# One adaLN transformer layer in split fp32r products: the second copy of k's high parts by DMA, and pair 0 of the heads split too

## The chip, the cores and the metric

The kernel runs on one core of a Trainium2 chip. The metric is the device time of one execution in microseconds; smaller is better. The core has TensorE (PE, with its weight loads shown apart as PEld), VectorE (DVE), ScalarE (ACT), GpSimd (POOL) and SyncE (SP, which here only issues DMAs). Every engine works through its own list of instructions in order and waits on semaphores.

## The reference, cut to what matters

There are 16 batches of 256 tokens with 128 features, 16 query heads of 64, and 4 key and value heads (4 query heads share one).

```
h = layernorm(x) * (1 + ca) + sa
q, k, v = h @ Wq, h @ Wkv;  q, k = rotary(q), rotary(k)
attn = softmax(q @ k.T / 8)               # per head, 256 x 256
x = x + ga * ((attn @ v) @ Wo + bo)
h = layernorm(x) * (1 + cb) + sb
x = x + gb * (gelu(h @ bin(w1).T + b1) @ bin(w2).T + b2)
```

`bin(w)` is the sign of w times the mean of its absolute values by row; `ga` and `gb` are made from a small conditioning matrix.

## The kernel before, in words

All work is float32 or float32r (a reduced float32 that TensorE multiplies faster). Where plain precision is wanted of float32r, an operand is cut into a **high** part (its value rounded to float32r) and a **low** part (the rest), and the product is made of high times high, high times low and low times high.

**Steps.** `attention_steps` (L155 to L166) runs one step for each batch, with the projections of the next batch (`prep`) and the output projection of the batch before (`out`) in the same step. There are 16 steps with attention, one ahead of them that only prepares, and a tail. The feed-forward part follows (`mlp_step`), partly beside the tail. All engines run the same step bodies.

**Slots.** A step has eight slots, and `SLOTS` (L60 to L69) is an order of work written by hand: slot 0 is

```
"S0 s4 s5 m s6 m s7 xT0 xT0 m m S1 m qt4 qt4 m mT1 qt4 qt4",
"S0 m s8 S1 m qkv02 qt5 qt5 qt5 qt5 qkv12 m m m m",
```

with slot 1 under it. PE goes through the words in order. ACT, DVE and POOL go through the same words and do what follows from each on their engine; of a unit that has several parts they act at its last word. A word is one of these:

- `S0`, `S1`: the transposed scores of one pair of heads (pair = slot number), one half of the keys each (`scores`, L962 to L976): two fp32r products, L972 and L974, into one of two banks `score_ps`. ACT then takes the exponential into `probs` (L648), and for a pair in `SPLIT_PAIRS` (L131) once more into `probs_hi` (L651); POOL makes `probs_lo` by subtraction (L515).
- `m`: one part of the product of the pair *of the slot before* with v (`product_with_v`, L978 to L1002), six words a pair. A plain pair uses the first and the fourth word only, with one plain fp32 product each (L989). A split pair uses all six with one fp32r product each (L999), two of `probs_hi` with `v_hi`, two with `v_lo`, two of `probs_lo` with `v_hi`; the last two wait for POOL. `SPLIT_PAIRS` is (1, 3, 4, 5, 7), so pairs 0, 2 and 6 are plain.
- `kt0`, `kt1`, `qt0` to `qt7`: PE turns k and q by identity products (L926). ACT copies q into `q_hilo` (L582), and k's high part **twice**, into the lower and the upper 64 partitions of `k_hi2` (the loop over `half` at L576 and L577), and its low part into `k_lo1` (L579). The upper copy is there because q's high and low parts lie on 128 partitions and both meet k's high part.
- `s0` to `s15`: one head's scores (L937), of which DVE takes the row maxima (L758); `s8` is the first to use `qt4` and waits for it (L933); `s0` and `s8` also wait for `k_hi2` (L934, L935). `mT0` to `mT3`: the maxima of four heads are turned (L941), and ACT copies them (L589).
- `qkv..`: projections (L911 to L913), then rotary terms on DVE (L748, L750), POOL (L501, L505) and ACT (L600). `xT0`: the normalised tokens turned (L903), then ACT (L564, L567) and DVE (L734).
- `bc..`, `yT..`, `zT0`: the reciprocals of the softmax sums spread by a product (L947) and applied on DVE (L763), the output projection (L953), and its turning back. `recip0` and `recip1` are DVE's reciprocals (L776 to L781).

A slot begins on ACT with the copy `o_un` of a finished pair (L657). Units use four banks `unit_ps` in turn; a unit waits for the reader of the one four before (`wait_for_reader`, L869).

**SP's list** in a step (L442 to L460) is: `maxima` of quarter 1, `gather_sums` 1, `high_parts` 2, `spread_reciprocals` 1, `maxima` 2, `high_parts` 3, `maxima` 3, `gather_sums` 0, `spread_reciprocals` 0, then for the next batch `high_parts` 0, `maxima` 0, `high_parts` 1. `high_parts` copies q's high parts of four heads into `q_him` (L419, 256 KB), `maxima` puts the turned maxima beside them (L425), `gather_sums` and `spread_reciprocals` lay the softmax sums and their reciprocals out over partitions (L432, L439). Each waits for what it copies and holds up what stands behind it.

Of the kernel before, what the change touches and what calls it, by code (L numbers as in the profile page):

```python
# [29 lines left out]
F32 = mybir.dt.float32  # L30
# [5 lines left out]
P = 128  # L36
# [91 lines left out]

SIGNS_AT = 4

SPLIT_PAIRS = (1, 3, 4, 5, 7)  # L131


class Step:
# [128 lines left out]
def adaln_layer(nc, x, wq, wkv, wo, bo, w1, b1, w2, b2, c, wmod, cos, sin, out):  # L263
    ctx = ExitStack()
    with ctx:
# [109 lines left out]
            sem("v_hi_ready"), sem("rot_parts"), sem("rot_summed"), sem("rot_high"), sem("rot_ready"))  # L375
        k_hi_ready, k_lo_ready, q_ready = sem("k_hi_ready"), sem("k_lo_ready"), sem("q_ready")
        q_him_in = [sem(f"q_him_in{i}") for i in range(4)]
        ident_r_ready, select_ready = sem("ident_r_ready"), sem("select_ready")
        neg_max_zero, max_ready, max_t_ready = sem("neg_max_zero"), sem("max_ready"), sem("max_t_ready")
        scores_full, probs_ready, pv_done = sem("scores_full"), sem("probs_ready"), sem("pv_done")  # L380
# [15 lines left out]
        @block.sync  # L396
        def _(sp):
            sp.dma_start(c_sb[:, :], c).then_inc(c_in, 16)
            sp.dma_start(xa[:, 0, :, :], x[0].rearrange("(c p) d -> p c d", p=P)).then_inc(x0_in, 16)
            sp.dma_start(wmod_sb, wmod).then_inc(wmod_in, 16)  # L400
            sp.dma_start(w_all[:, 0:INNER], wq).then_inc(wq_in, 16)
            sp.dma_start(w_all[:, INNER:WIDE], wkv).then_inc(wq_in, 16)
            sp.dma_start(cos_sb[:, :, :], cos.rearrange("(c p) d -> p c d", p=P)).then_inc(rope_in, 16)
            sp.dma_start(sin_sb[:, :, :], sin.rearrange("(c p) d -> p c d", p=P)).then_inc(rope_in, 16)
            sp.dma_start(bo_sb[:, :], bo.rearrange("(p o) -> p o", o=1)).then_inc(bias_in, 16)
            sp.dma_start(b2_sb[:, :], b2.rearrange("(p o) -> p o", o=1)).then_inc(bias_in, 16)
            for k in range(KF):
                sp.dma_start(b1_sb[:, k:k + 1], b1[k * P:(k + 1) * P].rearrange("(p o) -> p o", o=1)).then_inc(bias_in, 16)
            sp.dma_start(w1_sb[:, :, :], w1.rearrange("(k p) d -> p k d", p=P)).then_inc(ffw_in, 16)
            sp.dma_start(w2_sb[:, :], w2).then_inc(ffw_in, 16)  # L410
            for b in range(1, B, 5):
                sp.dma_start(xa[:, b:b + 5, :, :], x[b:b + 5].rearrange("b (c p) d -> p b c d", p=P)).then_inc(x_in, 16)
            sp.dma_start(wo_sb[:, :, :], wo.rearrange("(s p) n -> p s n", p=P)).then_inc(wo_in, 16)

            def high_parts(st, quarter, batch):


                sp.wait_ge(q_ready, st.count(8, 2 * quarter + 2, batch))
                sp.dma_start(q_him[quarter % 2][0:DH, :, :].bitcast(F32),  # L419
                             q_hilo[st.par(batch)][0:DH, 4 * quarter:4 * quarter + 4, :].bitcast(F32)).then_inc(q_him_in[quarter], 16)  # L420

            def maxima(st, quarter, batch):

                sp.wait_ge(max_t_ready, st.count(4, quarter + 1, batch))
                sp.dma_start(q_him[quarter % 2][DH:DH + 1, :, :].bitcast(F32).rearrange("o h (c i) -> o (h c) i", c=C),  # L425
                             neg_max_t[quarter % 2][:, :].bitcast(F32)).then_inc(q_him_in[quarter], 16)

            def gather_sums(st, half, batch):


                sp.wait_ge(o_un_ready, st.count(8, 4 * half + 4, batch))
                sp.dma_start(sums[:, :], o_un[DH:DH + 1, 4 * half:4 * half + 4, :, :]  # L432
                             .rearrange("o s h (b t) -> o (s h b) t", t=16)).then_inc(sums_in[half], 16)

            def spread_reciprocals(st, half, batch):

                sp.wait_ge(recip_lo_ready, st.count(2, half + 1, batch))
                for first, part in ((0, recip_hi), (32, recip_lo)):
                    sp.dma_start(recip_parts[half][first:first + PAIRS, :].bitcast(F32).rearrange("h (b t) -> h b t", t=16),  # L439
                                 part[:, :].bitcast(F32)).then_inc(recip_in[half], 16)  # L440

            def step(st):  # L442
                if st.attn:
                    maxima(st, 1, 0)
                if st.out:
                    gather_sums(st, 1, -1)
                if st.attn:
                    high_parts(st, 2, 0)
                if st.out:
                    spread_reciprocals(st, 1, -1)  # L450
                if st.attn:
                    maxima(st, 2, 0)
                    high_parts(st, 3, 0)
                    maxima(st, 3, 0)
                    gather_sums(st, 0, 0)
                    spread_reciprocals(st, 0, 0)
                if st.prep:
                    high_parts(st, 0, 1)
                    maxima(st, 0, 1)
                    high_parts(st, 1, 1)  # L460

            attention_steps(sp, step)

            with sp.Fori(0, B // 2) as t:
                for odd in range(2):
                    sp.wait_ge(y_ready, t * 2 + (odd + 1))
                    sp.dma_start(out[bass.ds(t * 2 + odd, 1)].rearrange("b (c p) d -> p (b c) d", p=P),
                                 y_sb[odd][:, :, :]).then_inc(y_out[odd], 16)
            for odd in range(2):
                sp.wait_ge(y_out[odd], 16 * (B // 2))  # L470
# [72 lines left out]
        def _(act):  # L543
# [12 lines left out]
            def unit(st, place, u):  # L556
                kind, ps, par = u[0], (tail_ps if st.tail else unit_ps)[bank(st, place)], st.par(ahead(u))
                if kind in ("s", "zT", "bc") or (kind == "qkv" and u[2] != 2) or u == ("yT", 0):
                    return
                act.wait_ge(unit_full, nth_unit(st, place))  # L560
                if kind == "xT":

                    b = st.batch(1)
                    act.activation(h_t[:, :], ps[:, 0:N], ACT.Identity, scale=mod[:, 1, bass.ds(b, 1)],  # L564
                                   bias=mod[:, 0, bass.ds(b, 1)]).then_inc(h_ready, 1)
                    act.wait_ge(h_ready, st.count(1, 1, 1))
                    act.activation(h_hi[0][:, :], h_t[:, :], ACT.Copy).then_inc(h_hi_ready, 1)  # L567
                if kind == "qkv":
                    act.activation(v_whole[par][:, u[1], :, 0:DH],
                                   ps[:, 256:512].rearrange("p (g d) -> p g d", g=KV), ACT.Copy)  # L570
                    act.activation(v_hi[par][:, u[1], :, 0:DH],
                                   ps[:, 256:512].rearrange("p (g d) -> p g d", g=KV), ACT.Copy).then_inc(v_hi_ready, 1)
                if kind == "kt":

                    high = ps[0:DH, :].rearrange("p (g i) -> p g i", g=2)
                    for half in range(2):  # L576
                        act.activation(k_hi2[par][half * DH:half * DH + DH, 2 * u[1]:2 * u[1] + 2, :], high,  # L577
                                       ACT.Copy).then_inc(k_hi_ready, 1)
                    act.activation(k_lo1[par][0:DH, 2 * u[1]:2 * u[1] + 2, :],  # L579
                                   ps[DH:P, :].rearrange("p (g i) -> p g i", g=2), ACT.Copy).then_inc(k_lo_ready, 1)  # L580
                if kind == "qt":
                    act.activation(q_hilo[par][:, 2 * u[1]:2 * u[1] + 2, :],  # L582
                                   ps[:, :].rearrange("p (h i) -> p h i", h=2), ACT.Copy).then_inc(q_ready, 1)
                if kind == "mT":
                    quarter = u[1]
                    if st.number != (-1, 0, None, None)[quarter]:

                        act.wait_ge(q_him_in[(quarter - 2) % 4], st.count(32, -32 if quarter < 2 else 0, ahead(u) + 1))
                    act.activation(neg_max_t[quarter % 2][:, :], ps[0:4 * C, 0:P], ACT.Copy).then_inc(max_t_ready, 1)  # L589
                if kind == "yT":  # L590

                    b = st.batch(-1)
                    act.activation(z_sb[:, :], ps[:, 0:N], ACT.Identity, scale=mod[:, 2, bass.ds(b, 1)],
                                   bias=ga_bo[:, bass.ds(b, 1)]).then_inc(z_ready, 1)
# [263 lines left out]
        def _(pe):  # L858
# [32 lines left out]
            def unit(st, place, u, part, last):  # L891
# [37 lines left out]
                if kind == "s":  # L929
# [2 lines left out]
                    if h % 2 == 0:  # L932
                        pe.wait_ge(q_ready, st.count(8, h // 2 + 1, ahead(u)))  # L933
                    if h % 8 == 0:  # L934
                        pe.wait_ge(k_hi_ready, st.count(4, h // 4 + 2, ahead(u)))  # L935
                    for ch in range(C):
                        ins = pe.matmul(ps[:, ch * N:(ch + 1) * N], q_hilo[par][:, h, ch * P:(ch + 1) * P],  # L937
                                        k_hi2[par][:, g, :], start=True, stop=True)
# [167 lines left out]
```

## Time and profile before

| what | value |
|---|---|
| median of 3 runs (711.74 to 713.76) | 713.3 us |
| the profiled execution, its own time | 712.71 us |
| its span in the profile | 710.9 us |
| PE busy | 672.1 us, 95% of the span |
| ACT busy | 551.4 us, 78% |
| DVE busy | 515.1 us, 72% |
| POOL busy | 430.6 us, 61% |
| mean granted TensorE clock | 0.978 |

The span is what the trace shows; 1.8 us of the execution's own time lie around it. A matmul's row starts when it enters the array's pipeline and ends when its last result is out, so neighbouring rows overlap, and the distance between two starts is what a matmul costs. A plain fp32 matmul stands as two rows.

### The profile page before, as it was taken

Reading aid. Unit: us, or ns where it says so; the run is one execution under the profiler, and the core shown is the slowest. Engines: PE = TensorE matmul, PEld = TensorE weight load, DVE = VectorE, ACT = ScalarE, POOL = GpSimd, SP = SyncE. Lnnn points to the kernel's source line nnn. Section 1 sums busy time; section 2 is a strip of 40 time slices with the busy share of each in tenths; the row PEclk is TensorE's granted clock in tenths of the full one; section 3 lists DMA queues with packets and bytes.
Section 4 is the critical chain, followed back from the end, with each engine's and each line's share of the span. In section 5 each row is a group of like instructions: output and inputs, shape, how many; then the busy total and the mean of one; then the engine's idle time right before and its main releaser. Section 6 shows DMA issues by size and latency. Waiting matters only on the chain.

```text
span 710.9 us, 13528 instructions
## 1 busy us (share of the span) xinstructions
PE 672.1 (95%) x3733; PEld 523.1 (74%) x3733; DVE 515.1 (72%) x1195; ACT 551.4 (78%) x1148; POOL 430.6 (61%) x397
## 2 busy tenths in 40 slices
PE   3488999999999999999999999999999999997897
PEld 3366777777878787878777777778777878666786
DVE  5556787887777777777787878777777777657673
ACT  3558887878788788878788878787887878766586
POOL 0447675867767676858576758577676768452110
PEclk9679999999999999999999999999999999998999
DMA  8011111111111111110201111111101111100111
GB/s 239 13 31 31 33 33 32 32 34 31 28 30 22 31 31 32 29 33 16 46 17 31 31 32 31 31 31 31 30 18 32 31 34 32 33 17 9 31 38 45
DMA packets 31580, 24.75 MB, mean 35 GB/s; under 512 B 16688, under 2 KB 26944, under 8 KB 31552
## 3 DMA queue, kind: packets, MB, share of 16 engines
q1 hardware_dynamic: 31552, 24.40, 16.3%
q8 instruction: 14, 0.23, 0.1%
q14 instruction: 14, 0.11, 0.1%
HBM read 4.47 MB, written 2.10 MB: 9 GB/s over the span
## 4 chain that ended last, share of the span: by engine, by line
PE 89%; DVE 3%; ACT 2%; issue 1%; POOL 1%; DMA 1%; SPq 0%; DVEq 0%; POOLq 0%
PE o_ps L999 15%; PE o_ps L989 11%; PE unit_ps L937 9%; PE score_ps L972 8%; PE score_ps L974 8%; PE unit_ps L926 8%; PE unit_ps L953 8%; PE o_ps L1054 4%; PE unit_ps L911 3%; PE unit_ps L912 3%; PE unit_ps L913 3%; PE unit_ps L947 2%; PE unit_ps L941 2%; DVE o_t L763 1%; PE unit_ps L1032 1%
## 5 line engine op out<-in xcount | busy, mean ns | idle before, releaser
L515 POOL TENSOR_TENSOR probs_lo<-probs,probs_hi 128x512 fp32r<-128x512 f32 x160 | 202.4, 1284 | 72.5 <-ACT probs_hi L651 72.5
L758 DVE TENSOR_REDUCE w_all<-unit_ps 128x2 f32<-128x512 f32 x256 | 166.0, 685 | 51.9 <-PE unit_ps L937 50.4
L501 POOL TENSOR_TENSOR rot_sum<-rot_a,rot_b 128x512 f32<-128x512 f32 (+1 forms) x96 | 104.8, 1098 | 106.7 <-DVE rot_b L750 106.5
L648 ACT ACTIVATE probs<-score_ps 128x512 f32<-128x512 f32 x256 | 150.5, 588 | 20.6 <-PE score_ps L974 18.0
L505 POOL TENSOR_TENSOR qk_rot<-rot_sum,qk_rot 128x512 fp32r<-128x512 f32 (+1 forms) x96 | 105.1, 1102 | 36.0 <-ACT qk_rot L600 36.0
L937 PEld LDWEIGHTS unit_ps<-k_hi,q_hilo 128*128 128x128 f32 x512 | 89.1, 192 | 42.8 <-issue 18.5
L937 PE MATMUL unit_ps<-k_hi,q_hilo 128*128 128x256 f32 x512 | 118.3, 319 | 2.1 <-ACT q_hilo L582 1.6
L972 PE MATMUL score_ps<-q_hilo,k_hi 128*128 128x512 f32 x256 | 113.4, 443 | 1.6 <-DMA q_him<-neg_max_t 1.6
L926 PEld LDWEIGHTS unit_ps<-ident_r,qk_rot 128*128 128x128 f32 x640 | 102.0, 194 | 16.9 <-issue 4.6
L926 PE MATMUL unit_ps<-ident_r,qk_rot 128*128 128x128 f32 x640 | 109.7, 263 | 4.5 <-POOL qk_rot L505 4.2
L763 DVE TENSOR_TENSOR o_t<-o_un,unit_ps 64x256 f32<-64x256 f32 x248 | 103.5, 417 | 5.7 <-PE unit_ps L947 1.3
L974 PE MATMUL score_ps<-q_him,k_lo 65*128 65x512 f32 x256 | 102.0, 398 | 0.0
L989 PE MATMUL o_ps<-probs,v_whole 128*65 128x512 f32 x192 | 98.1, 592 | 0.0
L651 ACT ACTIVATE probs_hi<-score_ps 128x512 fp32r<-128x512 f32 x160 | 94.1, 588 | 0.0
L582 ACT ACTIVATE q_hilo<-unit_ps 128x512 fp32r<-128x512 f32 x128 | 76.2, 596 | 8.5 <-PE unit_ps L926 8.3
L657 ACT ACTIVATE o_un<-o_ps 65x512 f32<-65x512 f32 x128 | 74.3, 581 | 1.9 <-PE o_ps L999 1.0
L748 DVE TENSOR_TENSOR rot_a<-unit_ps,cos_sb 128x512 f32<-128x512 f32 (+1 forms) x96 | 57.2, 596 | 24.0 <-PE unit_ps L941 16.8
L972 PEld LDWEIGHTS score_ps<-q_hilo,k_hi 128*128 128x128 f32 x256 | 48.8, 191 | 16.9 <-issue 9.3
L999 PE MATMUL o_ps<-probs_hi,v_hi 128*65 128x512 f32 x160 | 60.3, 395 | 0.0
L999 PE MATMUL o_ps<-probs_hi,v_lo 128*65 128x512 f32 x160 | 59.8, 411 | 0.0
L953 PE MATMUL unit_ps<-o_t,wo_sb 128*128 128x128 f32 x480 | 59.4, 277 | 0.0
L600 ACT ACTIVATE qk_rot<-rot_sum 128x512 fp32r<-128x512 f32 (+1 forms) x96 | 52.3, 561 | 8.5 <-POOL rot_sum L501 8.5
(119 smaller groups left out, 1128.7 us busy)
## 6 DMA issues: line engine op xcount, KB each, us to landing
q_him<-q_hilo SPq DMA_DIRECT2D x64, 256.0 KB
out_x<-w_all SPq DMA_DIRECT2D x16, 128.0 KB, 1.8
xa<-in_L_attn_x SPq DMA_DIRECT2D x3, 640.0 KB, 7.6
q_him<-neg_max_t SPq DMA_DIRECT2D x64, 4.0 KB
w_all<-in_L_attn_Wq SPq DMA_DIRECT2D x1, 512.0 KB, 4.4
w_sb<-in_L_ffn_w SPq DMA_DIRECT2D x2, 256.0 KB, 2.9
wo_sb<-in_L_attn_Wo SPq DMA_DIRECT2D x1, 512.0 KB, 7.8
sums<-o_un SPq DMA_DIRECT2D x32, 8.0 KB, 2.1
```

Source lines behind the costliest of these rows:

```text
L505: pool.tensor_tensor(low, total, high.bitcast(F32), ALU.subtract).then_inc(rot_ready, 1)
L515: pool.tensor_tensor(probs_lo[s % 2][:, jc, :, :], probs[s % 2][:, jc, :, :], probs_hi[s % 2][:, jc, :, :].bitcast(F32), ALU.subtract).the ...
L648: ins = act.activation(probs[s % 2][:, jc, :, :].rearrange("p h i -> p (h i)"), score_ps[jc][:, :], ACT.Exp, scale=SCALE)
L758: dve.tensor_reduce(neg_max[u[1] // 4][:, first:first + C], ps[:, :].rearrange("p (c j) -> p c j", c=C), AX.X, ALU.max, negate=True).then_ ...
L763: ins = dve.tensor_tensor(o_t[h * DH:h * DH + DH, u[1], :], o_un[0:DH, u[1], h, :], ps[h * DH:h * DH + DH, 0:N], ALU.mult)
L926: ins = pe.matmul(ps[:, part * P:(part + 1) * P], qk_rot[:, ch, first + h, :, :].rearrange("p t d -> p (t d)"), ident_r[:, :], start=True, ...
L937: ins = pe.matmul(ps[:, ch * N:(ch + 1) * N], q_hilo[par][:, h, ch * P:(ch + 1) * P], k_hi2[par][:, g, :], start=True, stop=True)
L953: ins = pe.matmul(ps[:, own], wo_sb[:, s, :], o_t[:, s, own], start=s == 0, stop=s == PAIRS - 1)
L972: pe.matmul(ps[:, :], k_hi2[par][:, g, js], q_hilo[par][:, hs, :].rearrange("p h i -> p (h i)"), start=True, stop=False)
L974: pe.matmul(ps[:, :], k_lo1[par][:, g, js], q_him[s // 2 % 2][:, s % 2 * 2:s % 2 * 2 + 2, :].rearrange("p h i -> p (h i)"), start=False, s ...
L989: ins = pe.matmul(o_ps[i][0:DH + 1, :], v_whole[par][:, jc, g, :], probs[i][:, jc, :, :].rearrange("p h i -> p (h i)"), start=jc == 0, sto ...
L999: ins = pe.matmul(o_ps[i][0:DH + 1, :], v[par][:, jc, g, :], p[i][:, jc, :, :].rearrange("p h i -> p (h i)"), start=part == 0, stop=part == 5)
```

## The change

`SPLIT_PAIRS` gets pair 0. ACT writes k's high part once, to the lower 64 partitions, and SP copies it to the upper 64 by one DMA for each of kt0 and kt1, with semaphores of their own. On SP's list the two DMAs stand behind `maxima` 3 and ahead of `gather_sums` 0. `s0` and `s8` wait for them instead of ACT's copies. A split pair's waits on POOL count 12 for a step in place of 10.

```
-SPLIT_PAIRS = (1, 3, 4, 5, 7)
+SPLIT_PAIRS = (0, 1, 3, 4, 5, 7)
...
+        k_twice_in = [sem(f"k_twice_in{i}") for i in range(2)]
...
+            def double_high_k(st, half, batch):
+
+                sp.wait_ge(k_hi_ready, st.count(2, half + 1, batch))
+                sp.dma_start(k_hi2[st.par(batch)][DH:P, 2 * half:2 * half + 2, :].bitcast(F32),
+                             k_hi2[st.par(batch)][0:DH, 2 * half:2 * half + 2, :].bitcast(F32)).then_inc(k_twice_in[half], 16)
...
                     maxima(st, 2, 0)
                     high_parts(st, 3, 0)
                     maxima(st, 3, 0)
+                if st.prep:
+                    double_high_k(st, 0, 1)
+                    double_high_k(st, 1, 1)
+                if st.attn:
                     gather_sums(st, 0, 0)
                     spread_reciprocals(st, 0, 0)
...
-                    for half in range(2):
-                        act.activation(k_hi2[par][half * DH:half * DH + DH, 2 * u[1]:2 * u[1] + 2, :], high,
-                                       ACT.Copy).then_inc(k_hi_ready, 1)
+                    act.activation(k_hi2[par][0:DH, 2 * u[1]:2 * u[1] + 2, :], high, ACT.Copy).then_inc(k_hi_ready, 1)
...
-                        pe.wait_ge(k_hi_ready, st.count(4, h // 4 + 2, ahead(u)))
+                        pe.wait_ge(k_twice_in[h // 8], st.count(16, 16, ahead(u)))
```

## Rows read from the trace of the kernel before

**Rows 1.** The page: busy times, and the chain that ended last by engine

```profile
PE 672.1 (95%) x3733; PEld 523.1 (74%) x3733; DVE 515.1 (72%) x1195; ACT 551.4 (78%) x1148; POOL 430.6 (61%) x397
...
PE 89%; DVE 3%; ACT 2%; issue 1%; POOL 1%; DMA 1%; SPq 0%; DVEq 0%; POOLq 0%
```

**Rows 2.** The chain in order of time, slots 1 and 2: start, length, what

```profile
311.14 0.86 PE o_ps L989 x2
312.00 0.24 PE unit_ps L937 x2
...
316.11 0.23 PE o_ps L999
```

**Rows 3.** Timeline, ACT in slot 0 and into slot 1: start, length

```profile
309.02 0.56 ACT L564 ACTIVATE h_t<-unit_ps,mod 128x256 f32<-128x256 f32 x1 [1.48 <-PE unit_ps L903]
...
309.94 0.58 ACT L648 ACTIVATE probs<-score_ps 128x512 f32<-128x512 f32 x1
...
310.56 0.27 ACT L589 ACTIVATE neg_max_t<-unit_ps 8x128 fp32r<-8x128 f32 x1
...
310.74 0.57 ACT L582 ACTIVATE q_hilo<-unit_ps 128x512 fp32r<-128x512 f32 x1
...
311.69 0.57 ACT L648 ACTIVATE probs<-score_ps 128x512 f32<-128x512 f32 x1
...
312.17 0.57 ACT L651 ACTIVATE probs_hi<-score_ps 128x512 fp32r<-128x512 f32 x1
```

**Rows 4.** Timeline: PE waits for q in slot 0; its products in slot 1

```profile
306.00 0.58 ACT L582 ACTIVATE q_hilo<-unit_ps 128x512 fp32r<-128x512 f32 x1
...
306.72 0.53 PEld L937 LDWEIGHTS unit_ps<-k_hi,q_hilo 128*128 128x128 f32 x4 [0.41 <-ACT q_hilo L582]
...
307.30 0.40 PE L999 MATMUL o_ps<-probs_hi,v_hi 128*65 128x512 f32 x1
...
310.98 1.02 PE L989 MATMUL o_ps<-probs,v_whole 128*65 128x512 f32 x2
...
312.07 0.40 PE L972 MATMUL score_ps<-q_hilo,k_hi 128*128 128x512 f32 x1
```

**Rows 5.** Timeline of the step after: the same exponential, q copy and L972

```profile
347.62 0.58 ACT L648 ACTIVATE probs<-score_ps 128x512 f32<-128x512 f32 x1
...
348.40 0.60 ACT L582 ACTIVATE q_hilo<-unit_ps 128x512 fp32r<-128x512 f32 x1
...
349.84 0.39 PE L972 MATMUL score_ps<-q_hilo,k_hi 128*128 128x512 f32 x1
```

**Rows 6.** Timeline, POOL from slot 0 to slot 1

```profile
307.88 1.29 POOL L505 TENSOR_TENSOR qk_rot<-rot_sum,qk_rot 128x512 fp32r<-128x512 f32 x1
312.82 2.54 POOL L515 TENSOR_TENSOR probs_lo<-probs,probs_hi 128x512 fp32r<-128x512 f32 x2 [3.66 <-ACT probs_hi L651]
```

**Rows 7.** Timeline, slots 4 to 6: ACT's k copies, SP's issues, DVE's reciprocals

```profile
327.26 1.22 ACT L577 ACTIVATE k_hi<-unit_ps 64x512 fp32r<-64x512 f32 x2
...
331.26 0.68 SPq L425 DMA_DIRECT2D q_him<-neg_max_t  x1
...
332.06 0.55 SPq L432 DMA_DIRECT2D sums<-o_un  x1
...
334.13 0.26 DVE L776 RECIPROCAL recip<-sums 128x16 f32<-128x16 f32 x1 [0.62 <-DMA sums<-o_un]
...
334.82 2.54 POOL L515 TENSOR_TENSOR probs_lo<-probs,probs_hi 128x512 fp32r<-128x512 f32 x2
...
334.92 1.22 DVE L780 TENSOR_TENSOR recip_lo<-recip,recip_hi 128x16 fp32r<-128x16 f32 x1
...
336.55 0.69 DVE L758 TENSOR_REDUCE w_all<-unit_ps 128x2 f32<-128x512 f32 x1 [0.41 <-PE unit_ps L937]
...
337.61 0.53 SPq L419 DMA_DIRECT2D q_him<-q_hilo  x1
```

**Rows 8.** By windows: busy PE, PEld, DVE, ACT, POOL; clock; DMA share, GB/s

```profile
339.00:339.50 0.50, 0.50 (x3) 0.32 (x2) 0.50 (x2) 0.00 (x0) 0.50 (x1) 1.00 1.09 213
```

## The prediction, made before the change was run

> **What bounds the kernel now.** I read the page first: PE is busy 95% of the span and makes 89% of the chain that ended last [rows 1], so only what changes PE's order of work in time counts. The same eight slots come back in each of 16 steps, so I then read one step: the chain in order of time [rows 2], and beside it the timelines of ACT, PE and POOL around slots 0 and 1, where the changed products stand [rows 3, 4, 6], the same place one step later [rows 5], and slots 4 to 6, where the copies of k stand [rows 7, 8]. The reader is to see two things. In slots 0 and 1 PE is never idle in the chain. But the work that PE waits for there comes only just in time: the q copy that s8 needs ends on ACT at 311.31 (310.74 + 0.57) [rows 3], while PE is still in pair 0's plain product, which began at 310.98 and holds it until s8 starts, 0.24 ahead of the L972 at 312.07 [rows 2, 4]. The slow product hides ACT.
>
> All sums below are made against the profiled execution, 712.71 us, of which 710.9 are its span. It stands 0.6 under the median of the runs, 713.3, and inside their spread.
>
> **PE's work.** Removed in a step: two plain products of pair 0, at 0.86 each in the chain, 1.72. Added: six fp32r products at 0.23, 1.38 [rows 2]. PE has 0.34 less to do, 5.4 in 16 steps. By the Trainium skill, FP8 and Floating Point Precision, section TensorE Precision Notes, true fp32 takes four passes of the array; two products would then be worth eight of the 0.23 passes, not 7.5 of them (1.72 / 0.23), and PE's relief would be 0.46 a step, 7.4 in all, by an estimate from that page. I keep the measured 0.86.
>
> **Where that work stands.** The first plain product stands ahead of s8, the second behind it. After the change one part stands ahead of s8 (0.23) and five behind it (5 x 0.23 = 1.15 in place of 0.86, so 0.29 more). So PE is 0.63 early at s8, and what counts is whether s8's operand is there.
>
> **ACT ahead of s8.** Pair 0 now needs a second exponential for each half of the keys. The first half's lies in the 1.48 that ACT idles ahead of h_t at 309.02 [rows 3]: nothing, and 0.48 if that idle time were gone. The second half's comes directly behind the exponential at 309.94, and ahead of the maxima's copy and the q copy that s8 waits for. Two exponentials follow each other at 0.48 (311.69 and 312.17). So: probs_hi at 310.42, the maxima's copy at 310.90, the q copy 0.18 behind it (310.56 to 310.74) at 311.08, done at 311.65 [rows 3].
>
> **From there to PE.** In slot 0 of the step PE does wait for a q copy, which gives the price: the copy ends at 306.58 and the load starts at 306.72, 0.14 later; four matmuls of L937 then take 0.58 until the next start at 307.30, the first load being bare, so two take 0.34 (0.58 less 0.24) [rows 2, 4]. So s8's load starts at 311.79 and the L972 behind it at 312.13, against 312.07 now: 0.06 late. In the step after, the exponential starts at 347.62, so the q copy at 348.76 (+0.48 + 0.48 + 0.18), ends at 349.36, and L972 starts at 349.84, just as now [rows 5]. Steps of these two kinds alternate; mean 0.03 late. The 0.63 that PE gained ahead of s8 is all waited away.
>
> **Behind s8.** The 0.29 more is then in the open, since nothing in the chain there but PE ends a wait. A step gets 0.03 + 0.29 = 0.32 longer; 16 steps give 5.1. Bounds: the link from q copy to L972 as measured, 0.48 in all, could be 0.1 shorter or longer in this place, 0.22 to 0.42 a step, so 3.5 to 6.7.
>
> **Part 0's own wait.** It now waits for the second probs_hi, which ends at 310.99 (310.42 + 0.57), so its load is at 311.13, against 310.98 for the product now [rows 3, 4]. It takes 0.23 and is done well ahead of s8's 311.79: nothing, and it would cost 0.15 if s8 did not wait longer.
>
> **ACT after s8.** ACT is 0.34 late (311.08 against 310.74), and its next work follows scores that PE makes 0.03 to 0.32 late itself; both move together, and I cost it at nothing. Behind it stand the o_un copy, slot 1's exponentials and SP's maxima of quarter 1; the latter are first used in slot 2, and I cost that at nothing too.
>
> **POOL.** Two more subtractions a step, 1.27 each (2.54 for two), 41 in 16 steps, on an engine that is busy 430.6 [rows 1, 6]. POOL is done with L505 at 309.17 and idles until 312.82. The first subtraction runs from 309.17 to 310.44, the second from about 311.1, when its probs_hi is there, to 312.4; the products that use them stand last in slot 1, nine fp32r products of 512 columns behind the L972 at 312.13 (part 1, six of the projections, parts 2 and 3), so not ahead of 314.2. Nothing on the path; up to 1.27 if POOL were not idle there. DVE's h_lo comes to lie beside the first subtraction and may be held up by it, up to 1.27, as recip_lo is in [rows 7]; it is not used before slot 1's first projection, so nothing.
>
> **The k copies.** ACT loses two copies of 0.61 a step (1.22 for two) [rows 7]. ACT's row count so stays as it was: two exponentials come for two copies, in other slots. ACT is 2% of the chain [rows 1], and in slots 4 and 5 of the steps I read PE follows PE, so this relief is worth nothing on PE; a gain is not excluded, and I bound it by that 2%, 14 us, of which I take nothing because none of it lies in these slots. SP gets two issues between the maxima of quarter 3 (331.26) and the sums (332.06). The nearest row is the copy of q's high parts, 256 KB in one issue of 0.53 [rows 7], moved at 213 GB/s [rows 8], so 1.2; the two k copies together carry as many bytes. Two issues put the sums back by 1.06; but the maxima's copy and o_un on ACT, which SP waits for, come 1.22 earlier. So the maxima are issued at 330.04, the k copies from 330.72, the sums at 331.8, 0.3 ahead of now, and they may queue behind the 1.2 of the k copies: they land between 333.9 and 334.5, where DVE now has them at 334.13 (332.06 + 2.07). DVE has 0.41 idle behind its reciprocals [rows 7], so nothing. The k copies themselves are issued by 331.8 and, at the sums' 2.07 and their own 1.2, land by 335.1 at the latest; s0's maxima start at 336.55, and s8 is in the next step: nothing. Without ACT's 1.22 the sums would be 1.06 late or more, which is the last rival.
>
> **Sum.** 712.7 + 5.1 = 717.8: slower, by 0.7%. Own range 715.5 to 720.
>
> **Rivals.** *Faster:* s8 finds its q copy ready, and PE keeps its 0.34 a step: 712.7 - 5.4 = 707.3. It decides at the q copy's end: to keep all, that must come by 310.7 or so (311.31 less 0.63). For it speaks that PE is 89% of the chain and has less to do. Against it, even today's 311.31 is too late. The Trainium skill's four passes would make this rival 705.3, by an estimate from the same page; the trace's 0.86 speaks against it.
>
> *No change:* ACT's extra exponential is hidden and q ends at 311.31 as now. Then the load is at 311.45 and L972 at 311.79, 0.28 early; with the 0.29 behind it the step is as long as before: 712.9. The timeline speaks against it [rows 3], since only 0.04 lies between the exponential's end (310.52) and the next start. What ACT is relieved of in slots 4 and 5 could give it no more here, since it idles 1.48 in between.
>
> *Slower still:* the sums are late after all, by the 1.06 of two issues or more. DVE's recip_lo takes 1.22 at 334.92 and ends with POOL's first subtraction (334.82 + 1.27 = 336.09); starting over 1.06 later, it would meet the second and end at 337.36, and the maxima that start at 336.55 would be 0.8 late [rows 7]. The Trainium skill, SBUF — State Buffer, section Summary: rules for kernel authors, says that of a DVE operation with two SBUF inputs and a GpSimd one the later blocks until the other is finished; the row agrees. Between 0 and 0.8 a step of it reaches PE; with 0.4 and 16 steps, 717.8 + 6.4 = 724.2. That the two DMAs don't do what ACT's copies did is no separate case: if they come late, s0 waits, and this rival prices it.
>
> **Chances.** Forecast 0.68; no change 0.14; faster 0.11; slower still 0.07. A measurement of this kernel tells 0.3%, 2.1 us, from no change. Some of the forecast's low end and all of the no-change case fall within it. So faster 0.11, same 0.16, slower 0.73. The range leaves out the faster rival and the slowest case, and takes in no change: 711.5 to 722.
>
> **What would show it.** Right: L989 loses a third of its rows, L999 and POOL's L515 gain a fifth; in slot 1 PE's load of L937 waits for ACT's L582, 16 times and some 0.5 each; a step takes 38.0 in place of 37.68 (309.94 to 347.62) [rows 3, 5]; the sums land as before. Wrong: no wait on L582 at s8 and a shorter step (the faster rival); a wait for DVE's L758 or for sums in slots 5 and 6 (slower still); a wait for POOL's L515 or for the k copy, which I cost at nothing.

## The result, and the profile after

| kernel | median | ratio to the kernel before | 95% interval |
|---|---|---|---|
| before | 712.83 us | | |
| after | 717.09 us | 1.0064 | 1.0048 to 1.0079 |

The change made the kernel slower by 0.6%, some 4.3 us by the medians. The profiled execution after took 716.65 us with a span of 714.9, which is 3.9 and 4.0 more than before; the granted clock was 0.978 in both.

The page of the kernel after: busy times, the chain by engine, three groups of instructions (busy, mean ns, idle before) and one DMA issue.

```profile
PE 672.7 (94%) x3765; PEld 526.9 (74%) x3765; DVE 516.4 (72%) x1195; ACT 546.1 (76%) x1148; POOL 470.6 (66%) x429
...
PE 84%; ACT 6%; DVE 3%; issue 3%; POOL 1%; DMA 1%; SPq 0%; ACTq 0%; DVEq 0%; POOLq 0%
...
L526 POOL TENSOR_TENSOR probs_lo<-probs,probs_hi 128x512 fp32r<-128x512 f32 x192 | 243.5, 1284 | 35.8 <-ACT probs_hi L660 35.8
...
L1008 PE MATMUL o_ps<-probs_hi,v_hi 128*65 128x512 f32 x192 | 73.5, 398 | 0.1
...
L998 PE MATMUL o_ps<-probs,v_whole 128*65 128x512 f32 x128 | 65.4, 592 | 0.0
...
k_hi<-k_hi SPq DMA_DIRECT2D x32, 128.0 KB, 2.2
```

Against [rows 1], ACT has 5 us less to do, but went from 2% of the chain to 6%, and "issue" from 1% to 3%: the span holds waits that it did not hold before. POOL has 40 us more.

Timeline of the kernel after, slots 0 and 1 of the step that [rows 3, 4] show of before (all lines stand 9 higher: L981 is the L972 of before, L946 the L937, L1008 the L999).

```profile
311.52 0.39 PE L981 MATMUL score_ps<-q_hilo,k_hi 128*128 128x512 f32 x1
...
311.58 1.28 POOL L526 TENSOR_TENSOR probs_lo<-probs,probs_hi 128x512 fp32r<-128x512 f32 x1
...
312.40 0.58 ACT L657 ACTIVATE probs<-score_ps 128x512 f32<-128x512 f32 x1
...
312.53 0.61 DVE L743 TENSOR_TENSOR h_lo<-h_t,h_hi 128x256 fp32r<-128x256 f32 x1
...
312.88 0.59 ACT L660 ACTIVATE probs_hi<-score_ps 128x512 fp32r<-128x512 f32 x1
...
313.36 0.25 ACT L598 ACTIVATE neg_max_t<-unit_ps 8x128 fp32r<-8x128 f32 x1
...
313.51 0.57 ACT L591 ACTIVATE q_hilo<-unit_ps 128x512 fp32r<-128x512 f32 x1
...
313.59 0.13 PEld L1008 LDWEIGHTS o_ps<-probs_hi,v_hi 128*65 128x65 f32 x1 [0.44 <-issue]
...
314.21 0.30 PEld L946 LDWEIGHTS unit_ps<-k_hi,q_hilo 128*128 128x128 f32 x2 [0.48 <-issue]
314.21 0.49 PE L946 MATMUL unit_ps<-k_hi,q_hilo 128*128 128x256 f32 x2 [0.17 <-ACT q_hilo L591]
...
314.54 0.40 PE L981 MATMUL score_ps<-q_hilo,k_hi 128*128 128x512 f32 x1
...
315.01 0.40 PE L1008 MATMUL o_ps<-probs_hi,v_hi 128*65 128x512 f32 x1
```

The new exponential stands at 312.88 between the old one and the maxima's copy. The q copy follows at 313.51 and ends at 314.08, and s8's load starts at 314.21: PE waited, both for part 0's operand (313.59) and for s8's (314.21). The view puts these waits of the loads down to "issue", because here an instruction of PE's sequencer ahead of the load carries the wait: the one with the wait for q starts at 314.121, 0.04 behind the copy's end. The same stretch before:

```profile
309.06 0.39 PE L972 MATMUL score_ps<-q_hilo,k_hi 128*128 128x512 f32 x1
```

From this product of slot 0 to slot 1's own (312.07 in [rows 4]) PE took 3.01; after it takes 314.54 - 311.52 = 3.02, with 0.63 less work in it. In the steps between it takes 3.02 before and 2.87 after.

To compare kernels I take the length of a step: the distance between the starts of xT0's second product in the fourth and in the fourteenth step that has one, over ten. The ten steps hold both kinds in equal number. Each ratio stands against runs of the kernel before on the same chip: 712.83 us for after, 713.28 for e1, e2, e3 and e5, 712.26 for e4, e6, e7 and e8, 712.72 for e9 and e8b.

| kernel | starts, us | step, us | median, us | ratio (95%) |
|---|---|---|---|---|
| before | 119.76, 497.17 | 37.74 | | |
| after | 120.73, 501.35 | 38.06 | 717.09 | 1.0064 (1.0048 to 1.0079) |
| e1_k_dma_alone | 120.51, 498.87 | 37.84 | 714.41 | 1.0017 (1.0008 to 1.0026) |
| e2_pair0_alone | 120.62, 500.83 | 38.02 | 716.97 | 1.0050 (1.0036 to 1.0064) |
| e3_s8_later | 120.79, 497.15 | 37.64 | 710.56 | 0.9968 (0.9955 to 0.9981) |
| e5_one_exp_less | 120.67, 498.47 | 37.78 | 713.43 | 1.0008 (0.9997 to 1.0018) |
| e4_s8_later_before | 119.61, 496.94 | 37.73 | 712.02 | 1.0001 (0.9991 to 1.0011) |
| e6_k_dma_one_wait | 119.16, 496.34 | 37.72 | 712.61 | 1.0007 (0.9997 to 1.0017) |
| e7_part0_sooner | 119.09, 494.24 | 37.52 | 708.59 | 0.9950 (0.9935 to 0.9965) |
| e8_all_three | 119.44, 493.61 | 37.42 | 707.88 | 0.9935 (0.9920 to 0.9950) |
| e9_k_by_act | 118.87, 493.04 | 37.42 | 708.07 | 0.9932 (0.9918 to 0.9946) |
| e8b_all_three_again | 119.88, 494.00 | 37.41 | 708.79 | 0.9935 (0.9922 to 0.9949) |

### The profile page after: what moved, and what is told of

Read it like the earlier page. It is cut to its first block, busy times and chain, and to the rows that moved or that the text cites. A ratio compares the mean times of both kernels' runs of the same rounds, so it can differ in the third digit from the quotient of the medians.

```text
span 714.9 us, 13740 instructions
## 1 busy us (share of the span) xinstructions
PE 672.7 (94%) x3765; PEld 526.9 (74%) x3765; DVE 516.4 (72%) x1195; ACT 546.1 (76%) x1148; POOL 470.6 (66%) x429
## 4 chain that ended last, share of the span: by engine, by line
PE 84%; ACT 6%; DVE 3%; issue 3%; POOL 1%; DMA 1%; SPq 0%; ACTq 0%; DVEq 0%; POOLq 0%
PE o_ps L1008 16%; PE unit_ps L946 10%; PE unit_ps L962 8%; PE score_ps L981 8%; PE score_ps L983 7%; PE o_ps L998 7%; PE unit_ps L935 7%; PE o_ps L1063 4%; PE unit_ps L920 3%; PE unit_ps L921 3%; PE unit_ps L922 3%; PE unit_ps L956 2%; PE unit_ps L950 1%; ACT probs L657 1%; DVE o_t L772 1%
## 5 line engine op out<-in xcount | busy, mean ns | idle before, releaser
L526 POOL TENSOR_TENSOR probs_lo<-probs,probs_hi 128x512 fp32r<-128x512 f32 x192 | 243.5, 1284 | 35.8 <-ACT probs_hi L660 35.8
L946 PEld LDWEIGHTS unit_ps<-k_hi,q_hilo 128*128 128x128 f32 x512 | 88.0, 192 | 42.8 <-issue 14.5
L946 PE MATMUL unit_ps<-k_hi,q_hilo 128*128 128x256 f32 x512 | 113.5, 310 | 5.7 <-ACT q_hilo L591 3.7
L660 ACT ACTIVATE probs_hi<-score_ps 128x512 fp32r<-128x512 f32 x192 | 113.1, 589 | 0.0
L981 PE MATMUL score_ps<-q_hilo,k_hi 128*128 128x512 f32 x256 | 106.8, 417 | 0.8 <-DMA q_him<-neg_max_t 0.8
L1008 PE MATMUL o_ps<-probs_hi,v_hi 128*65 128x512 f32 x192 | 73.5, 398 | 0.1
L1008 PE MATMUL o_ps<-probs_hi,v_lo 128*65 128x512 f32 x192 | 69.8, 408 | 0.0
L1008 PE MATMUL o_ps<-probs_lo,v_hi 128*65 128x512 f32 x192 | 66.0, 394 | 0.0
L998 PE MATMUL o_ps<-probs,v_whole 128*65 128x512 f32 x128 | 65.4, 592 | 0.0
```

What stands on the lines that cost most here:

```text
L526: pool.tensor_tensor(probs_lo[s % 2][:, jc, :, :], probs[s % 2][:, jc, :, :], probs_hi[s % 2][:, jc, :, :].bitcast(F32), ALU.subtract).the ...
L660: ins = act.activation(probs_hi[s % 2][:, jc, :, :].rearrange("p h i -> p (h i)"), score_ps[jc][:, :], ACT.Exp, scale=SCALE)
L981: pe.matmul(ps[:, :], k_hi2[par][:, g, js], q_hilo[par][:, hs, :].rearrange("p h i -> p (h i)"), start=True, stop=False)
L998: ins = pe.matmul(o_ps[i][0:DH + 1, :], v_whole[par][:, jc, g, :], probs[i][:, jc, :, :].rearrange("p h i -> p (h i)"), start=jc == 0, sto ...
L1008: ins = pe.matmul(o_ps[i][0:DH + 1, :], v[par][:, jc, g, :], p[i][:, jc, :, :].rearrange("p h i -> p (h i)"), start=part == 0, stop=part == 5)
```

## The experiments

The theory was the forecast's: PE's gain is lost at s8, which waits for ACT's q copy behind the new exponential, and what stands behind s8 is then longer.

**Each half of the change alone.** e1 keeps pair 0 plain; e2 leaves k's copies on ACT.

```
e1, from after:  -SPLIT_PAIRS = (0, 1, 3, 4, 5, 7)   +SPLIT_PAIRS = (1, 3, 4, 5, 7)
e2, from before: -SPLIT_PAIRS = (1, 3, 4, 5, 7)      +SPLIT_PAIRS = (0, 1, 3, 4, 5, 7)
```

> The k copies go by DMA; pair 0 stays plain. Theory (the loss is pair 0's alone, the k copies are off PE's path both ways): as the kernel before, 712.8 us within 1, ratio 0.999 to 1.001; the sums of quarter 0 still land within 0.4 of now. Rival 1 (the two DMAs cost something on the path, such as the 0.11 a step that the changed kernel loses between slots 4 and 5): 714.5, ratio 1.0025, or more. Rival 2 (ACT's relief of two copies helps PE): under 711, ratio under 0.998.

> Pair 0 is split; ACT makes both k copies as before. Theory: the whole of the loss, 717.1 us, ratio 1.005 to 1.007, with s8's load waiting for ACT's q copy in slot 1 of each step. Rival 1 (the DMAs carry part of the loss): 715 to 716. Rival 2 (without ACT's relief in slots 4 and 5 ACT falls behind for good, being given 0.96 a step more and nothing less): over 720, and a step over 38.4.

Pair 0 alone makes a step 0.28 longer (38.02 - 37.74) and the time 1.0050 of before; most of the loss is here. The k copies, which I had costed at nothing, make a step 0.10 longer (37.84 - 37.74), a loss of 0.17%, small, but the interval leaves out no loss: the expectation missed there, and with 714.41 us its first rival came nearest. The two do not add up exactly: 0.28 + 0.10 is 0.38, and after has 0.32. Most of the difference lies in every second step, where e2 takes 2.94 from slot 0's second scores to slot 1's and after 2.87. In these steps s8's load starts 0.12 behind the q copy's end in e2 and 0.05 in after. In e2 an instruction ahead of the load carries the wait for q, in after the load carries it itself; what such a difference costs is read below, at mT3.

**s8 moved behind the scores.** If s8 is the place of the loss, PE should do something else there. Slot 1's second `S1` needs nothing new, so it goes first.

```
-    "S0 m s8 S1 m qkv02 qt5 ...
+    "S0 m S1 m s8 qkv02 qt5 ...
```

> The changed kernel with one word of slot 1 moved: s8 stands behind S1 and the second m, so that PE has three scores and products more to do before it needs the q copy. Theory (PE's gain is waited away at s8 and nowhere else): L981 of slot 1 comes 0.5 to 0.6 earlier, a step takes some 37.45, and the time is 707 to 708.5, ratio 0.992 to 0.994 to the kernel before. Rival 1 (ACT, not s8's place, sets the pace in slots 0 to 2): the wait turns up at S1's exponentials or at s9 and s10 instead, and the time stays at 716 to 718. Rival 2 (part of the wait moves to part 0, which needs the second probs_hi): 709 to 712.

Timeline of e3, slots 0 and 1:

```profile
309.43 0.40 PE L981 MATMUL score_ps<-q_hilo,k_hi 128*128 128x512 f32 x1
...
310.78 0.59 ACT L660 ACTIVATE probs_hi<-score_ps 128x512 fp32r<-128x512 f32 x1
...
311.41 0.57 ACT L591 ACTIVATE q_hilo<-unit_ps 128x512 fp32r<-128x512 f32 x1
...
311.49 0.13 PEld L1008 LDWEIGHTS o_ps<-probs_hi,v_hi 128*65 128x65 f32 x1 [0.43 <-issue]
...
311.78 0.39 PE L981 MATMUL score_ps<-q_hilo,k_hi 128*128 128x512 f32 x1
...
312.25 0.42 PEld L946 LDWEIGHTS unit_ps<-k_hi,q_hilo 128*128 128x128 f32 x2
...
312.71 0.40 PE L920 MATMUL unit_ps<-w_hi,h_hi 128*128 128x512 f32 x1
```

ACT does exactly what it did: the q copy stands 1.98 behind slot 0's product (311.41 - 309.43) and 1.99 in after. But s8's load at 312.25 has no wait any more. The step is 0.42 shorter than after's, and the kernel is faster than before, 0.9968. The theory's 37.45 a step and 708.5 us at most were missed, and the second rival, 709 to 712 us, came: one wait is left, at part 0 (311.49), 0.12 behind the new exponential's end.

**One exponential less.** The rival was that not ACT's exponential, but the six products themselves or POOL's subtraction hold the slot up. e5 is after without the new second-half exponential.

```
-                            if s in SPLIT_PAIRS:
+                            if s in SPLIT_PAIRS and (s > 0 or jc == 0 or st.number == 0):
```

> The changed kernel, but in all steps except the first ACT leaves out the second half's exponential into probs_hi for pair 0, and the products and POOL take what that buffer still holds. So the split products are all there and ACT has its old 0.48 ahead of the q copy back. Theory: the q copy ends 0.34 earlier at s8 and L981 of slot 1 comes 0.2 to 0.3 earlier, a step is as long as before, 712.9 us, between 712 and 714 (ratio 0.999 to 1.002). Rival 1 (the extra exponential is not what delays s8): 717. Rival 2 (without it PE keeps its whole relief): 707.5.

Timeline of e5, the same stretch:

```profile
310.04 0.39 PE L981 MATMUL score_ps<-q_hilo,k_hi 128*128 128x512 f32 x1
...
311.54 0.27 ACT L598 ACTIVATE neg_max_t<-unit_ps 8x128 fp32r<-8x128 f32 x1
...
311.71 0.57 ACT L591 ACTIVATE q_hilo<-unit_ps 128x512 fp32r<-128x512 f32 x1
...
312.41 0.30 PEld L946 LDWEIGHTS unit_ps<-k_hi,q_hilo 128*128 128x128 f32 x2 [0.55 <-issue]
...
312.76 0.39 PE L981 MATMUL score_ps<-q_hilo,k_hi 128*128 128x512 f32 x1
```

All products and subtractions are still there, and the q copy comes 0.32 sooner (1.67 behind slot 0's product, not 1.99). PE's next scores follow by 0.30 (2.72, not 3.02), and the step is 0.28 shorter than after's. So ACT's list ahead of the q copy sets this slot. It does not come 0.48 sooner, because the maxima's copy then stands directly behind the end of the one exponential (310.91 + 0.58 = 311.49, copy at 311.54), as it did before [rows 3], and not 0.48 behind the start of another; s8 still waits, and the kernel stands where it stood before, 1.0008: what the forecast's "no change" rival describes. Its step, 37.78, still holds the 0.10 that the k copies cost (e1).

**Was the place of s8 good for something by itself?** e4 is the kernel before with the same move of s8.

> The kernel before, with s8 moved behind S1 and the second m as in the third experiment. Theory (before the change nothing waits at s8, since the plain product covers the q copy): no gain, 712 to 714 us, ratio 0.999 to 1.002. Rival (the move is worth something by itself, whatever pair 0 is): 710 to 711, ratio 0.997 or less, as the changed kernel gained 0.43 a step from it.

It makes no difference, 1.0001. Before, PE's plain product hid ACT, so e3's gain is not a gain that the kernel before could have had.

**Why the k copies cost.** In e1 nothing waits for k's DMAs, which land 2.2 us after their issue, and DVE waits 14.6 us in all for the sums, 13.6 before, which is not on PE's path. What its trace does show is a longer way between slots 4 and 5, at mT3, in the steps of the loop. First before, then e1: DVE's maxima, and PE's load behind them.

```profile
326.78 1.29 DVE L758 TENSOR_REDUCE w_all<-unit_ps 128x2 f32<-128x512 f32 x2
...
328.12 0.14 PEld L941 LDWEIGHTS unit_ps<-ident,w_all 128*128 128x128 f32 x1 [0.33 <-DVE w_all L758]
```

```profile
327.93 1.29 DVE L767 TENSOR_REDUCE w_all<-unit_ps 128x2 f32<-128x512 f32 x2
...
329.34 0.14 PEld L950 LDWEIGHTS unit_ps<-ident,w_all 128*128 128x128 f32 x1 [0.39 <-DVE w_all L767]
```

Before, the load starts 0.05 behind DVE's end (326.78 + 1.29 = 328.07), in e1 0.12 (329.22 to 329.34). The trace also holds the instructions of PE's sequencer, which the views leave out. The wait of mT0 to mT3 for the maxima is at L940 (L949 in the other kernels here). Over all of them, the instructions of that line are:

```
          ALU_OP   EVENT_SEMAPHORE      the one ahead of the load shown (e6: below)
before    48       16                   ALU_OP, 32 ns, at 327.507
e1        36       28                   EVENT_SEMAPHORE, 51 ns, at 329.262
after     36       28
e6        48       16                   ALU_OP, 32 ns, at 326.808
```

Both the ALU_OP and the load wait on the semaphore that DVE's maxima raise. Before, the ALU_OP, an instruction on a register, started at 327.507, 0.04 behind the end of s14's maxima (326.78 + 0.69, the first of the two in DVE's line) and 0.56 ahead of the end of s15's. So it waited for s14's, whose bank mT3 takes, and the wait for the last maxima was the load's own. In e1 the ALU_OP is gone at mT3, in all 12 steps of the loop. The wait for the last maxima is now an instruction of its own, of 51 ns, which starts 0.04 behind their end, and the load comes behind it. The kernel before holds both forms: outside the loop, where the counts are constants, the wait stands by itself too (the 16 in its row), and in the three last steps with attention mT3's load starts 0.115 behind the maxima, with no k copy by DMA at all. The new counts of k's DMAs go up by 16 a step, as the maxima's does, so I took it that they share a register now. e6 gives both DMAs one semaphore, so that the count goes up by 32, and PE waits for it once, at s0.

```
-        k_twice_in = [sem(f"k_twice_in{i}") for i in range(2)]
+        k_twice_in = sem("k_twice_in")
...
-                    if h % 8 == 0:
-                        pe.wait_ge(k_twice_in[h // 8], st.count(16, 16, ahead(u)))
+                    if h == 0:
+                        pe.wait_ge(k_twice_in, st.count(32, 32, ahead(u)))
```

> The k copies by DMA alone, as in the first experiment, but with one semaphore for both, and PE waits for it once a step, at s0, with a count that goes up by 32 and not by 16 a step. The two DMAs are the same. Theory (the 0.11 a step between slots 4 and 5 is PE's own: with the count by 16 the wait of mT3 for the maxima became an instruction of its own between DVE's end and PE's load): the load follows DVE's end by 0.05 again, the step is 0.11 shorter than in the first experiment, 712.8 to 713.6 us, ratio 0.999 to 1.0010. Rival (the DMAs themselves, their issues or their traffic, cost the 0.11): 714.4, ratio 1.0015 to 1.002, and the load stays 0.12 behind DVE's end.

The DMAs are all there, the counts of the table above are again those of before, and so are the step (37.72) and the time (1.0007). In e6 the load starts 0.05 behind DVE's end:

```profile
326.08 1.29 DVE L767 TENSOR_REDUCE w_all<-unit_ps 128x2 f32<-128x512 f32 x2
...
327.42 0.14 PEld L950 LDWEIGHTS unit_ps<-ident,w_all 128*128 128x128 f32 x1 [0.33 <-DVE w_all L767]
```

So the loss is the wait's form and not the copy. That a shared register is what changes the form is argued from the counts and e6, not shown.

**Taking away what is left.** e7 is e3 with part 0 of pair 0 waiting for the first half's exponentials only, which are all that it multiplies. e8 is e7 with e6's semaphore.

```
-                    pe.wait_ge(probs_ready, st.count(16, 2 * s))
+                    pe.wait_ge(probs_ready, st.count(16, 2 * s - (s == 1)))
```

> The third experiment (s8 later), and part 0 of pair 0's product waits for the first half's probs_hi alone, which is all that it reads; S1, which stands between parts 0 and 1, waits for the second half anyway. Theory (PE loses 0.14 a step at part 0, for the second probs_hi): PE's idle time ahead of part 0 goes, S1's stays under 0.05, a step is 0.1 to 0.14 shorter, 708.3 to 709.2 us, ratio 0.993 to 0.995. Rival 1 (S1 then waits for as long, since it reads the bank that the same exponential frees): 710.5. Rival 2 (ACT is the pace now and the gain comes back as a wait for pair 1's exponentials): 710 to 711.

> The changed kernel with s8 later, part 0's wait for the first half alone, and one semaphore for both k copies. Theory (three separate losses of PE, 0.43, 0.14 and 0.11 a step, and its work is 0.34 a step less than before): 707 to 708.3 us, ratio 0.991 to 0.994, a step of 37.4. Rival (the losses cover each other): 709 to 710.5.

Timeline of e8:

```profile
307.17 0.39 PE L981 MATMUL score_ps<-q_hilo,k_hi 128*128 128x512 f32 x1
...
308.84 0.14 PEld L1008 LDWEIGHTS o_ps<-probs_hi,v_hi 128*65 128x65 f32 x1
...
309.30 0.39 PE L981 MATMUL score_ps<-q_hilo,k_hi 128*128 128x512 f32 x1
...
309.78 0.40 PEld L946 LDWEIGHTS unit_ps<-k_hi,q_hilo 128*128 128x128 f32 x2
```

Neither part 0 nor s8 waits. The steps close the account: from after's 38.06, moving s8 takes 0.42 (37.64), part 0's wait 0.12 (37.52), the wait at mT3 0.10 (37.42). What is left is 0.32 under the 37.74 of before, and that is PE's own relief, forecast at 0.34. e8 beats both kernels, at 0.9935 of before.

**Is the DMA worth anything when PE no longer waits?** e9 is e7 with both k copies made by ACT and with PE's waits on them, as before; e8 was run again beside it (e8b).

```
-                    act.activation(k_hi2[par][0:DH, 2 * u[1]:2 * u[1] + 2, :], high, ACT.Copy).then_inc(k_hi_ready, 1)
+                    for half in range(2):
+                        act.activation(k_hi2[par][half * DH:half * DH + DH, 2 * u[1]:2 * u[1] + 2, :], high,
+                                       ACT.Copy).then_inc(k_hi_ready, 1)
...
-                double_high_k(st, 0, 1)
-                double_high_k(st, 1, 1)
```

> As the experiment with all three edits (707.9 us), but ACT makes both k copies, as before the change: pair 0 split, s8 later, part 0's wait for the first half alone. Theory (the k copies are off PE's path even when PE no longer waits in slots 0 and 1; the DMA copy is worth nothing): the same within what can be measured, ratio to the kernel before 0.992 to 0.995. Rival 1 (ACT, given 0.96 a step and relieved of nothing, now falls behind): 709.5 or more, ratio over 0.996, with PE or PE's loads waiting for ACT in slots 4 to 6. Rival 2 (without the two DMAs it is faster still): under 706.5.

> The kernel with all three edits once more, on the same chip as the one above, to be compared with it: 707 to 708.5 us, ratio 0.992 to 0.995 to the kernel before. Theory: within 0.7 us of the one above. Rival: 1.5 us or more under it.

e9 has 0.9932 and e8b 0.9935, with intervals that nearly coincide, and the steps are alike (37.42 and 37.41). By the medians e8b lies 0.72 above e9 and, at 708.79, 0.3 above its expected range; single runs of the two are spread over 1.6 and 2.0 us. ACT's relief of two copies a step is worth nothing that can be measured; the gain is the split of pair 0 alone, once its waits are out of the way.

## Why the prediction was right, and where its sum was not

Forecast 717.8, measured 717.09, and in the profiled execution 716.65; slower, as said, inside the range. The mechanism is the one forecast: PE's gain is waited away at s8. The terms held less well than the total; that a step's loss came out at just the 0.32 forecast is luck, since two errors of 0.10 cancel, one at the q copy and one at the k copies.

- **PE's relief, 0.34 a step:** right. e8 shows 0.32. The Trainium skill, FP8 and Floating Point Precision, section TensorE Precision Notes, has true fp32 at four passes, by which it would be 0.46 by the prediction's estimate. The trace does not bear the 0.46 out, and the measured 0.86 of [rows 2] does; it speaks against 0.23 as the price of a pass and not against the four, since a quarter of 0.86 is 0.215.
- **ACT ahead of s8:** right in kind, 0.1 too long on the mean. The sign named for it came: in each of the 16 steps s8's load starts 0.05 to 0.12 behind the q copy's end. In the step that starts at 308.49 before, the exponential to L972 was forecast as 0.48 + 0.48 + 0.18 + 0.57 + 0.14 + 0.34 = 2.19 and measured 2.14 (312.40 to 314.54); most of the difference is the maxima's copy to q copy, 0.15 for 0.18. In the steps between, forecast as 2.22 (347.62 to 349.84, [rows 5]), it took 2.07, by this timeline of after:

```profile
350.49 0.58 ACT L657 ACTIVATE probs<-score_ps 128x512 f32<-128x512 f32 x1
...
351.60 0.57 ACT L591 ACTIVATE q_hilo<-unit_ps 128x512 fp32r<-128x512 f32 x1
...
352.22 0.30 PEld L946 LDWEIGHTS unit_ps<-k_hi,q_hilo 128*128 128x128 f32 x2 [0.48 <-ACT q_hilo L591]
...
352.56 0.39 PE L981 MATMUL score_ps<-q_hilo,k_hi 128*128 128x512 f32 x1
```

  Here the q copy takes 0.57 where [rows 5] had 0.60, and s8's load starts 0.05 behind its end (352.17), where I had taken 0.14 from another place. That is the wait's form again: here the load itself carries the wait for q, in the other kind of step an instruction ahead of it does. From scores to scores the two kinds of step went from 3.01 to 3.02 and from 3.02 to 2.87. So the term 0.03 should have been (0.01 - 0.15) / 2 = -0.07; it lies within the 0.1 that I had allowed the link.
- **Behind s8, 0.29:** right; the order of the words leaves no other value, and in the rows of after PE waits for nothing from 314.54 to 316.4.
- **Part 0's own wait, costed at nothing:** right in this kernel, and the price that the prediction gave it if s8's wait were gone, 0.15, is what e7 shows, 0.12.
- **POOL:** right, no product of a step waits for L526 (the one wait for it, 0.5 in the tail, is there before too). DVE's h_lo beside it takes 0.61 in place of 0.43, and nothing waits for that.
- **The k copies, costed at nothing: the step that failed.** They cost 0.10 a step (e1), by neither of the things weighed, ACT's relief and the sums. It was the form of PE's own wait, at mT3, a place that the diff does not touch (e6). The sums' part was read rightly. Timeline of after, slots 4 to 6, against [rows 7]:

```profile
332.51 0.27 ACT L598 ACTIVATE neg_max_t<-unit_ps 8x128 fp32r<-8x128 f32 x1
...
332.80 0.68 SPq L426 DMA_DIRECT2D q_him<-neg_max_t  x1
333.59 1.16 SPq L446 DMA_DIRECT2D k_hi<-k_hi  x2
334.85 0.53 SPq L433 DMA_DIRECT2D sums<-o_un  x1
336.96 0.25 DVE L785 RECIPROCAL recip<-sums 128x16 f32<-128x16 f32 x1 [0.71 <-DMA sums<-o_un]
...
339.43 0.69 DVE L767 TENSOR_REDUCE w_all<-unit_ps 128x2 f32<-128x512 f32 x1 [0.54 <-PE unit_ps L946]
```

The maxima are issued 0.79 ahead of the k copies, whose two issues take 1.16, and the sums land 2.11 behind their own issue, as before (2.07). From the maxima's issue to the reciprocal it is now 4.16 and was 2.87, 1.29 more; but ACT, relieved of two copies, lets the maxima go 0.93 sooner in the step (22.77 behind the start of xT0's second product, now 21.84: 331.26 less 308.49, 332.80 less 310.96); that is the 1.22 of two copies less the 0.29 by which slot 1 got longer. The reciprocal so comes 0.36 later in the step, and DVE's next maxima, which follow PE, 0.41, so against PE's own lateness the sums are not late. DVE still waits for PE ahead of these (0.54, before 0.41), so the "slower still" rival did not come.

- **Sixteen equal steps:** too many. In the ten steps of the table the loss is 0.32 each, as it happens just the forecast: -0.07 + 0.29 + 0.10. In the last steps it is not. Timelines, last step with attention, before and after:

```profile
610.64 0.40 PE L972 MATMUL score_ps<-q_hilo,k_hi 128*128 128x512 f32 x1
...
612.31 0.27 ACT L589 ACTIVATE neg_max_t<-unit_ps 8x128 fp32r<-8x128 f32 x1 [0.42 <-PE unit_ps L941]
...
613.90 0.40 PE L972 MATMUL score_ps<-q_hilo,k_hi 128*128 128x512 f32 x1
```

```profile
615.11 0.39 PE L981 MATMUL score_ps<-q_hilo,k_hi 128*128 128x512 f32 x1
...
616.78 0.27 ACT L598 ACTIVATE neg_max_t<-unit_ps 8x128 fp32r<-8x128 f32 x1
...
617.96 0.40 PE L981 MATMUL score_ps<-q_hilo,k_hi 128*128 128x512 f32 x1
```

There ACT idled 0.42 for mT1 before, and the new exponential goes into that idle time: the stretch falls from 3.26 to 2.85, more than the 0.29 that follows. The rows show it; no run tested it. The two steps ahead of it gain alike (3.04 and 3.07 before, 2.77 and 2.76 after), and outside the loop mT3 loses nothing, since its wait stood by itself there already. This and the end behind the last scores, 0.4 shorter in after (span less the last L981: 74.1 against 74.5), bring the 5.1 of the forecast down to the 4.0 of the spans; the 0.4 is within what that end differs by from run to run (last section).

The faster rival did not come either, but e8 shows that it was three waits away: its 707.3 is close to what e8 measures (707.88), once s8, part 0 and mT3 no longer wait.

## What to carry to other kernels

A slow operation on the engine that bounds the kernel can be the cover of another engine's work. Before making it faster, look at how much later than needed that other engine's result comes; and if the answer is "just in time", reorder the bounding engine's words first, or the gain turns into a wait. When a part of a change that should be free costs a little in every step, compare the engines' sequencer instructions too: a new semaphore can change how a wait elsewhere is issued, and in these runs the wait that ends last was cheapest on the load that needs it.

## What the runs showed that was not expected

- A wait that the load itself carries and one on an instruction of its own ahead of the load are not the same: behind the same DVE maxima, PE's load starts 53 ns after their end in the one case and 116 ns in the other (medians over the steps; before and e1). The next load, yT0's, then follows 126 ns later and not 72, so that 2291 ns from the matmul ahead of mT3 to slot 5's first scores become 2402. That is 0.11 a step. Behind ACT's q copy it is the same, 52 and 123 ns (after, the two kinds of step at s8).
- DVE's h_lo, a subtraction of two SBUF operands, takes 612 ns on the mean beside POOL's subtraction in after and 425 in before. The Trainium skill, SBUF — State Buffer, section Summary: rules for kernel authors, says that of a DVE operation with two SBUF inputs and a GpSimd one that reads SBUF the later blocks until the first is finished. The trace agrees: in each of the 14 steps in which the two overlap, h_lo ends 0.28 to 0.29 us behind L526's end, however long the overlap (0.28 to 0.49), so that by these numbers some 0.14 of its own 0.43 are done ahead of that. In the step shown L526 ends at 312.86 (311.58 + 1.28) and h_lo at 313.14.
- The time from the last scores to the end of the span differs between runs whose kernels do not differ there: it is 73.8 (e9), 74.1 (after), 74.8 (e8) and 75.3 us (e2, and e8 run again). Differences below some 0.2% were therefore read from the steps, not from one span.
